# The value branch of layer 0: three groups of four by nine taps, small scalings as products of two tensors, and a new order on every engine

## The reference, cut to what matters

```python
hidden = einsum('bchw,oc->bohw', gn(x), w_hidden) + b_hidden      # 64 -> 384 channels
hidden = depthwise_conv3x3(hidden, w_dw) + b_dw
q, k, v = split(hidden, 3)                                        # 128 channels each
out = irfft2(rfft2(patches8x8(q)) * rfft2(patches8x8(k)))         # per 8 x 8 patch
out = (out - mean_c(out)) / sqrt(var_c(out) + 1e-5) * ln_w + ln_b
x = x + einsum('bchw,oc->bohw', v * out, w_proj) + b_proj
```

## Time and profile before

| what | value |
|---|---|
| median of 3 runs | 8754.44 us (8754.39 to 8754.59) |
| the profiled execution | 8754.59 us, its span 8752.8 us |
| PE busy | 8435.8 us, 96% of the span |
| DVE busy | 7480.2 us, 85% |
| ACT busy | 6324.6 us, 72% |
| POOL busy | 4840.4 us, 55% |
| mean granted TensorE clock | 0.993 |

### The profile page before, as it was taken

How to read it: one execution, slowest core, us unless ns; L and a number is a source line. 1 busy time by engine, 2 the same in 40 slices (tenths; PEclk the granted TensorE clock), 3 DMA queues, 4 the chain that set the end, 5 groups by cost and what they waited for, 6 DMA issues and landing times. The chain is left out here.

```text
span 8752.8 us, 169999 instructions
## 1 busy us (share of the span) xinstructions
PE 8435.8 (96%) x57716; PEld 4818.6 (55%) x57716; DVE 7480.2 (85%) x9839; ACT 6324.6 (72%) x8629; POOL 4840.4 (55%) x2723
## 2 busy tenths in 40 slices
PE   2999999999999999999999999999879999999999
PEld 1666666666666666666666666666323333333333
DVE  6888888888888888888888888888759999999998
ACT  2777777777777777777777777777208888888887
POOL 1444444444444444444444444444109999999998
PEclk9999999999999999999999999999999999999999
DMA  6222222222222222222222212212694555555554
GB/s 154 54 68 61 55 68 63 55 67 54 64 68 53 64 56 66 64 56 65 64 49 55 54 43 54 54 43 54 146 203 114 119 119 119 119 119 119 119 119 111
DMA packets 613650, 711.27 MB, mean 81 GB/s; under 512 B 44029, under 2 KB 572507, under 8 KB 589575
## 3 DMA queue, kind: packets, MB, share of 16 engines
q1 hardware_dynamic: 611022, 690.44, 33.9%
q10 hardware_dynamic: 2488, 18.98, 1.0%
HBM read 548.96 MB, written 164.11 MB: 81 GB/s over the span
## 5 line engine op out<-in xcount | busy, mean ns | idle before, releaser
L625 PE MATMUL banks<-w_hi,hi_lo 128*128 128x256 f16 x18432 | 2362.6, 273 | 35.1 <-DVE hi_lo L927 35.1
L625 PEld LDWEIGHTS banks<-w_hi,hi_lo 128*128 128x128 f16 x18432 | 1737.7, 98 | 844.9 <-issue 533.5
L583 POOL TENSOR_TENSOR u_im<-q_im,k_swap 128x512 f32<-128x512 f32 x512 | 741.3, 1448 | 1810.4 <-ACT q_im L821 1723.8
L959 DVE SCALAR_TENSOR_TENSOR v_s<-banks,tap_w,v_s 128x512 f32<-128x512 f32 x2048 | 1535.1, 750 | 55.0 <-ACT v_s L810 0.6
L1511 PE MATMUL banks<-z,conv_w 128*128 128x512 f32 x3096 | 1556.0, 618 | 1.2 <-ACT z L1639 1.2
L1482 POOL TENSOR_TENSOR part_sum<-part_sum,prod 128x1024 f32<-128x1024 f32 x645 | 1525.2, 2365 | 52.2
L795 ACT ACTIVATE qk<-banks,inv_wscale 128x512 f32<-128x512 f32 x1024 | 706.5, 690 | 910.2 <-PE banks L625 903.7
L586 POOL TENSOR_TENSOR u<-u,u_im 128x512 f32<-128x512 f32 x512 | 725.3, 1417 | 766.8 <-DVE u L936 766.8
L625 PE MATMUL banks<-w_lo_pair,hi_pair 128*128 128x256 f16 x6144 | 1006.1, 273 | 0.0
L592 POOL TENSOR_TENSOR u<-u,u_mean 128x512 f32<-128x512 f32 x512 | 532.2, 1040 | 733.7 <-DVE u_mean L967 733.7
L1511 PEld LDWEIGHTS banks<-z,conv_w 128*128 128x128 f32 x3096 | 521.5, 188 | 628.1 <-issue 570.5
(11 more groups left out here) (252 smaller groups left out, 15777.1 us busy)
## 6 DMA issues: line engine op xcount, KB each, us to landing
xr<-in_x_dram SPq DMA_DIRECT2D x258, 640.0 KB, 9.1
xb<-y_scratch SPq DMA_DIRECT2D x262, 320.0 KB, 4.7
xa<-y_scratch SPq DMA_DIRECT2D x262, 256.0 KB, 5.4
x_res<-in_x_dram SPq DMA_DIRECT2D x258, 256.0 KB, 4.1
out_dram<-res SPq DMA_DIRECT2D x258, 256.0 KB, 3.3
y_scratch<-ys SPq DMA_DIRECT2D x256, 256.0 KB, 3.9
prod<-y_scratch SPq DMA_DIRECT2D x256, 256.0 KB, 5.6
xs<-in_x_dram SPq DMA_DIRECT2D x92, 512.0 KB, 7.4
```

The source lines that it names most:

```text
L583: nc.gpsimd.tensor_tensor(u_im[:], q_im[:], k_swap[:], ALU.mult).then_inc(u_made, 1)
L625: r = pe.matmul(out, px, w, start=n == 0, stop=n == 13)
L959: v.scalar_tensor_tensor(v_out, hidden_v[:, 1 + dc:GCOL + 1 + dc, 1 + dr:R + 1 + dr], tap_w[:, t:t + 1], v_out, ALU.mult, ALU.add).then_in ...
```

## The change

Let `j` be a group's place in a body, counted in fours for each strip.

- **v.** Only the first group of each strip (`j % 4 == 0`) is convolved on PE (`value`). The other three go by `hidden`, `first_tap` and eight taps.
- **Indicator rows** (L910 before) are scaled only in the first two strips and next to an image's edge, 18 instructions in the program.
- **Small scalings on DVE** (`means`, `masks`, the copy in `params`) were a tensor times a number or a column. They become `tensor_tensor` products of two tensors in SBUF, with a tensor of 1/128 (`per_p`), of ones, or with the column broadcast.
- **The last addition of `output`** moves from DVE to POOL (`output_sum`). `t_n` is now waited for by name (`t_made`).
- **The order** on all engines is new. Taps are interleaved with other work on DVE; both halves of `low_parts` come behind the first group's complex sum on POOL; steps of a group come later relative to the convolutions. Wait counts are adapted, and a body is also run ahead of the first and twice behind the last, with what does not exist left out.

```diff
+            def tapped(i, j):
+                return i * 6 + (3 * (j // 4) + j % 4)
...
-                    if k % 2:
-                        middle_tap(i, k, not (first and k < 4))
+                        first_tap(i, j + 1)
...
+                        first_tap(i, j + 2)
...
+                        first_tap(i, j + 3)
...
-                    v.tensor_scalar(u_mean[:], u_mean[:], 1.0 / P, None, ALU.mult).then_inc(means_ready, 1)
+                        v.tensor_tensor(u_mean[:], u_mean[:], per_p[:, 0:4], ALU.mult).then_inc(means_ready, 1)
...
-                            last = v.tensor_scalar(xn[p0:p0 + C, :, slot], xn[p0:p0 + C, :, slot],
-                                                   par[b][p0:p0 + C, col:col + 1], None, ALU.mult)
+                                last = v.tensor_tensor(xn[p0:p0 + C, :, slot], xn[p0:p0 + C, :, slot],
+                                                       par[b][p0:p0 + C, col:col + 1].to_broadcast([C, W]), ALU.mult)
...
-                    for row, col in ((0, 4), (R - 1, 5)):
-                        v.tensor_scalar(hi_ind[b][C:P, 1:W + 1, row], ind[C:P, :, row], par[b][C:P, col:col + 1], None, ALU.mult)
+                        for row, col, edge in ((0, 4, 0), (R - 1, 5, S - 1)):
+                            if isinstance(s, int) and (s < 2 or s % S == edge or (s - 2) % S == edge):
+                                v.tensor_scalar(hi_ind[b][C:P, 1:W + 1, row], ind[C:P, :, row], par[b][C:P, col:col + 1], None, ALU.mult)
...
+                def output_sum(i, jp):
+
+                    if real_pair(i, jp):
+                        out = ys[jp // 2 % 2][:, :, GCOL * (jp % 2):GCOL * (jp % 2) + GCOL]
+                        pool.wait_ge(fin_read, i * 4 + (jp + 1))
+                        pool.wait_ge(t_made, i * 4 + (jp + 1))
+                        nc.gpsimd.tensor_tensor(out, out, t_n[:].rearrange("p (c r) -> p r c", r=R), ALU.add).then_inc(fin_step, 1)
...
+                def hidden(i, j, projected, then_forward=None):
+
+                    if real(i, j):
+                        if j % 4 == 1:
+                            pe.wait_ge(v_copied, i * 2 + (j // 4 + 1))
+                        else:
+                            pe.wait_ge(v_tapped, (tapped(i, j) - 1) * 8)
+                        need(pe, t_made, i * 4 + (projected + 1))
...
```

The new order on PE, for one strip (`h` is 0 or 1):

```diff
+                    for h in range(2):
+                        j, jp, js = 4 * h, 2 * h, h
+                        inverse(i, j - 2)
+                        project(i, jp - 2, j - 1)
+                        value(i, j, image if h == 0 else None, then_forward=j)
+                        forward(i, j)
+                        hidden(i, j + 1, jp - 2)
+                        tile(i, j + 1, 0)
+                        tile(i, j + 1, 1)
+                        inverse(i, j - 1)
+                        tile(i, j + 1, 2)
+                        tile(i, j + 1, 3)
+                        variance(i, jp - 1)
+                        tile(i, j + 2, 0)
+                        project(i, jp - 1, j + 1, then_forward=j + 1)
+                        forward(i, j + 1)
+                        tile(i, j + 2, 1)
+                        hidden(i, j + 2, jp - 1)
+                        tile(i, j + 2, 2)
+                        inverse(i, j)
...
+                        hidden(i, j + 3, jp - 1)
+                        inverse(i, j + 1)
+                        tile(i, j + 4, 0)
...
```

The new order on ACT, from a strip's first tap on:

```diff
+                        first_tap(i, j + 1)
+                        query_imaginary(i, j)
+                        key_swap(i, j)
+                        square(i, j - 1)
+                        query_real(i, j)
+                        qk_copy(i, j + 1, 0)
```

More of the change, by code:

```diff
@@ L578, in imaginary @@
[L578 to L586, removed]
@@ L607, in tail, with low_parts @@
[L607 to L614, removed]
+                def low_parts(i, js, half):
+                    if real_strip(i, js):
+                        s = i * 2 + js
+                        pool.wait_ge(hi_made, s + 1)
+                        need(pool, stacks_ready, s + 0)
+                        c0, c1 = W // 2 * half, W // 2 * half + W // 2
+                        nc.gpsimd.tensor_tensor(hl_all[C:P, 1 + c0:1 + c1, 1:SL], xn[C:P, c0:c1, 0:SL - 1],
+                                                hi_all[C:P, 1 + c0:1 + c1, 0:SL - 1], ALU.subtract).then_inc(low_made, 1)
+                        pool.wait_ge(low_made, s * 2 + (half + 1))
@@ L651, in conv_v @@
                     one(hi_side[b], -1, w_lo_one[:, 0, KQ:KV])
-                    before_last()
+                    if before_last:
+                        before_last()
                     return one(hi_ind[b], 0, w_lo_one[:, 1, KQ:KV])
[L655 to L665, removed]
@@ new lines, in value @@
+                def value(i, j, image=None, then_forward=None):
+                    if real(i, j):
+                        need(pe, v_tapped, tapped(i, j) * 8)
+                        if image is not None:
+                            averages(image)
+                        conv_v(j // 4 % 2, ORDER[0], None if then_forward is None else lambda: transform_ready(i, then_forward))\
+                            .then_inc(v_conv, 1)
+                    elif then_forward is not None:
+                        transform_ready(i, then_forward)
@@ new lines, in variance @@
+                def variance(i, jp, then_forward=None):
+                    if real_pair(i, jp):
+                        pe.wait_ge(sq_ready, i * 8 + (2 * jp + 2))
+                        need(pe, fin_read, i * 4 + jp)
+                        for h in range(2):
+                            if h and then_forward is not None:
+                                transform_ready(i, then_forward)
+                            last = pe.matmul(b_var[C * h:C * h + C, :], mean_w[:, 0:C], sq[h][:], start=True, stop=True)
+                        last.then_inc(var_done, 1)
+                    elif then_forward is not None:
+                        transform_ready(i, then_forward)
```

713 lines of the change are left out of this document (388 added, 325 removed).

## The result

The changed kernel takes **8937.69 us** (median of 4 runs, 8935.19 to 8947.74) against 8754.42 us for the kernel before: a ratio of 1.0214, with a 95% interval of 1.0201 to 1.0227. The forecast was 8601 us. It is 183 us slower where 154 us faster was forecast, so 337 us have to be found. The profiled execution has a span of 8945.9 us.

A forecast was written before the change was run, and what follows sets the result against it. PE's instruction stream was taken to bound layer 0. A strip saves 2.4 us of PE's work and loses 1.2 to a new wait: 128 x (2.4 - 1.2) = 154 us off 8754.6, giving 8601 us, range 8440 to 8700.

The forecast's parts named there:

- PE's own work: TensorE's instruction stream in layer 0: 44.4 us a strip without waits instead of 46.8, worth 307 us.
- The chain to `hidden(j+2)`: DVE's `scaled` behind the `hl_all` copy and `means`, delayed by POOL's `low_parts`: PE waits 1.2 us a strip.
- the step that the prediction called the most likely to be wrong: PE's wait of 1.2 us a strip at `hidden(j+2)`, the difference of two chains of 15 us.
- "No second wait ... 0.5 to spare": After `hidden(j+2)`: stacks complete at 28.7 us, wanted by PE at 29.2, so no further wait.
- third rival: DVE becomes the bound, meeting POOL for 9.8 us, 47 a strip: slower, about 8855 us; chance 0.10.
- fourth rival: No change, within 0.2% (17 us): a strip of 46.7 to 46.9 us, or PE's wait doubled; chance 0.05.
- the wait of 1.2 doubled: One way to no change: PE's wait of 1.2 us a strip at `hidden(j+2)` comes out twice as long.
- The form of the scalings: Two-tensor products for `masks` and `means` on DVE: worth nothing, since they still wait for POOL's running operation.
- DVE's load: DVE's time a strip: 40.3 + 6.0 - 2.2 - 3.7 = 40.4 us, 91% of 44.4.
- `output_sum`: The addition moved to POOL: 1.4 us taken, with 1.4 as lower and 2.3 us as upper bound.
- Image ends: PE waiting for DVE's variance at images' ends: no change taken, bounds +8 and -8 us each, three times.

The follow-up runs named there:

- e12: e10 with the four statistics of the next image's x dealt out two to each strip, not all in a body's first: 8399.9 us, ratio 0.9599.
- e1: The changed kernel with 40 idle waiting instructions ahead of TensorE's code of layer 0: 8768.8 us, ratio 1.0018 to the kernel before.
- e4: e1 with three of the nine taps of v left out in each strip's third group: 8497.5 us, ratio 0.9707 to the kernel before.
- e6: e1 with DVE's `params`, `high_below`, `shifted` and `both_stacks` among operations put in other places, same operations: 8566.5 us, ratio 0.9785.
- e8: e1 with POOL's `less_mean` between the two halves of `low_parts` instead of behind both: 8688.9 us, ratio 0.9924 to the kernel before.
- e9: e6 with `high_below` moved ahead of the first tap, into the gap where DVE stood idle: 8503.0 us, ratio 0.9713 to the kernel before.
- e10: e9 with the copy to `hi_pair` moved right behind `product(j)`: 8451.3 us, ratio 0.9654 to the kernel before.
- e5: e1 with the old forms of the small scalings (means, masks) and parameters as a copy again: 8777.7 us, ratio 1.0027 to the kernel before.
- e7: The kernel before with indicator rows scaled only near edges, one more single body per image and 90 idle instructions ahead: 8712.9 us, ratio 0.9954.

## Why the prediction was wrong, step by step

- **PE's own work: right.** 44.4 us a strip were reckoned without waits; 47.0 less 2.45 of waits is 44.55, and e12, where PE hardly waits, runs at 44.0.
- **The chain to `hidden(j+2)`: right in all its points.** With 0 at 2014.31, the end of `hidden(j+1)`: the taps of DVE end at 5.7 (5.6 reckoned), `product(j)` at 6.5 (6.6), POOL's half begins at 8.2 (8.2), `means` ends at 14.3 (14.6), `t_n` at 14.9 (15.3). PE's wait is 0.69 us, where 1.2 was reckoned. So the step that the prediction called the most likely to be wrong came out 0.5 us better than its sum, just under the range of 0.7 to 1.7.
- **"No second wait ... 0.5 to spare": this step failed.** PE wanted the stacks at 29.15 (29.2 reckoned; it had started `hidden(j+2)` 0.4 us earlier than reckoned, and the blocks from there took 0.3 longer), but they were complete at 30.7, not at 28.7. The chain from `t_n` on was not worked out with its waits: the taps ended at 27.2 instead of 26.2, because of the parameters (0.9 us of waiting) and `hi_ind` (0.8), and the three stack copies took 3.6 us instead of 2.5. My own third rival listed these waits ("the first stack copy", "parameters", "the next stacks"), but weighed them against DVE's total load, with a threshold of 46.8 us. The load stayed at 44.9. What counted was their place in the chain. The two waits, 0.69 and 1.76 us, are 2.45 us a strip: as much as the 2.4 that PE's shorter work had saved, and twice the 1.2 of the sum, (2.45 - 1.2) x 128 = 160 us. e1 is the kernel without the other loss: 168 us above the forecast, and no gain (1.0018). That is the fourth rival's case, "the wait of 1.2 doubled", which had a chance of 0.05. e4, e6, e8, e9, e10 and e12 show the chain to be the cause.
- **The fetching of TensorE's code: not foreseen at all.** It costs 169 us (medians of e1 and of the changed kernel). With e1's 168 us above the forecast these are the 337 us that had to be found.
- **The form of the scalings: right.** It is worth nothing (e5); `means` met POOL once a strip.
- **DVE's load: off by 4.5 us.** The waits at new places were left out, and the indicator scalings gave back 1.1 us instead of 3.7 (e7): I had counted a wait as work.
- **`output_sum`**: 1.53 us (1.4 taken, bounds 1.4 and 2.3). It lies where nobody waits for it. **Image ends**: the three long strips are 54.6, 53.8 and 53.7 us against 56.5, 58.0 and 55.3, within the bounds of 8 us.

## What to carry to other kernels

An engine that is 90% busy can bound a kernel by a chain long before its load does: follow the chain right round to the next point where the slowest engine waits, with every wait priced, and put small work into the gap ahead of the chain. An operation whose duration is mostly a wait may free little when it goes: here the next one inherited the wait. When a program's length changes, look at the instruction queue's packets by time before blaming the order: idle instructions that shift the code cost nothing to try, and gave 1.9% here.

## What the runs showed of the hardware

- A product of 128 x 4 numbers takes 0.15 us alone and 2.66 us beside a POOL subtraction of 64 x 1280 numbers, and the other forms fare alike: the means 0.79 us on average as a `tensor_scalar` against 0.78, the parameters 1.03 us as a copy against 1.02. The Trainium skill, "SBUF — State Buffer", section "Who interferes with whom", says that a DVE copy or `tensor_scalar` can contend with GpSimd, and a `tensor_tensor` with both inputs in SBUF does so with GpSimd's reads; the trace agrees.
- POOL's operations grow too where DVE's meet them: L605 takes 3012 ns in the changed kernel and took 2716, and the subtraction L630 that runs beside the copies to `hi_pair` and `hi_ind` takes 2.10 us where its shortest takes 1.04.
- A loop of TensorE can be fetched anew in each body: 87 packets before, 336 after, 111 with 40 idle instructions ahead, 535 with 230. Such a body lost 1 to 9 us. Part of it is the clock: 0.68 granted over the 10 us that hold the stalls, 1.00 over the 50 us before.
